# Extra TensorE products in a fused encoder: ahead of attention, in the last scan group, about its output product and at the feed-forward's entry

## The reference

```python
def reference(...):                      # 16 sequences, 36 image patches + 77 text tokens, 256 wide
    h = _L0_tok_ref(x, ...)              # patches @ W_proj.T + bias + position
    h = concatenate([h, txt], axis=1)    # (16, 113, 256)
    h = h + _L0_attn_ref(_layernorm(h), ...)   # causal attention, 16 heads of 16
    h = h + _L0_ffn_ref(_layernorm(h), ...)    # top-1 of 8 experts (256-512-256) + a shared expert
    h = h + _L1_attn_ref(_layernorm(h), ...)   # selective scan, below
    h = h + _L1_ffn_ref(_layernorm(h), ...)    # 704 hidden units, fake-quantised, below
    return h

def _L1_attn_ref(x, ...):
    x_in, res = jnp.split(x @ in_proj_w.T + in_proj_b, 2, axis=-1)
    xc = _silu(conv4(x_in))                                   # causal, 4 taps, per channel
    delta, Bp, Cp = jnp.split(xc @ x_proj_w.T + x_proj_b, [64, 80], axis=-1)
    delta = jax.nn.softplus(delta @ dt_proj_w.T + dt_proj_b)
    dA = jnp.exp(delta[..., None] * -jnp.exp(A_log))          # 16 states
    dBu = delta[..., None] * Bp[:, :, None, :] * xc[..., None]
    ys = scan(dA, dBu)                                        # over time
    y = ((ys * Cp[:, :, None, :]).sum(-1) + xc * D_param) * _silu(res)
    return y @ out_proj_w.T + out_proj_b + (x @ skip_proj_w.T + skip_proj_b)

def _L1_ffn_ref(x, ...):     # quantised to whole numbers: x, w_gate, w_up, then silu(gate)*up, w_down
    scale = sigmoid(clip) * max(abs(x)) / 127                 # one maximum over the whole tensor
    ...
```

## Time and profile before

| | us |
|---|---|
| median of 3 runs | 802.52 |
| lowest, highest | 800.22, 802.92 |
| profiled execution, first to last instruction | 798.0 |
| PE busy in it | 685.9 |
| DVE busy | 491.1 |
| ACT busy | 385.6 |
| POOL busy | 328.9 |

### The profile page before, as it was taken

How to read it: one execution, slowest core, us unless ns; L and a number is a source line. 1 busy time by engine, 2 the same in 40 slices (tenths; PEclk the granted TensorE clock), 3 DMA queues, 4 the chain that set the end, 5 groups by cost and what they waited for, 6 DMA issues and landing times. The chain is left out here.

```text
span 798.0 us, 11738 instructions
## 1 busy us (share of the span) xinstructions
PE 685.9 (86%) x3705; PEld 462.7 (58%) x3706; DVE 491.1 (62%) x885; ACT 385.6 (48%) x859; POOL 328.9 (41%) x310
## 2 busy tenths in 40 slices
PE   7599999997999979999996678898898896544886
PEld 5478888876666646666664556566566563312434
DVE  1556666665421114444225778898888988995586
ACT  0466666663222113333322666766766855211965
POOL 0012211110185403322321078878878878620337
PEclk9799999997799989999998899999999998865799
DMA  9993000000021261111114201202202202000003
GB/s 256 317 424 134 0 0 0 0 2 1 0 38 25 40 204 41 40 50 42 41 39 107 94 29 66 95 8 87 94 1 93 94 0 94 0 0 0 1 2 93
DMA packets 28836, 52.89 MB, mean 66 GB/s; under 512 B 10975, under 2 KB 23683, under 8 KB 26627
## 3 DMA queue, kind: packets, MB, share of 16 engines
q1 hardware_dynamic: 20067, 47.62, 17.8%
q0 software_dynamic: 8736, 4.85, 2.5%
HBM read 42.75 MB, written 9.60 MB: 66 GB/s over the span
## 5 line engine op out<-in xcount | busy, mean ns | idle before, releaser
L494 POOL TENSOR_TENSOR arena<-arena 128x904 f32<-128x904 f32 x64 | 124.8, 1950 | 66.6 <-DVE arena L1271 59.2
L1271 DVE TENSOR_TENSOR_SCAN arena<-ps,arena 128x452 f32<-128x452 f32 x128 | 133.7, 1087 | 11.6 <-POOL arena L494 4.4
L794 ACT ACTIVATE ps<-arena,sh_w 128x448 f32<-128x448 f32 x128 | 79.2, 632 | 94.9 <-DVE arena L1271 94.4
L1569 PE MATMUL ps<-arena,work 128*128 x176 | 83.4, 598 | 0.0
L569 ACT ACTIVATE work<-ps,work 113x113 f32<-113x113 f32 x256 | 66.8, 387 | 32.4 <-DVE work L928 32.4
L1261 DVE TENSOR_TENSOR arena<-arena,ps 128x904 f32<-128x904 f32 x64 | 69.0, 1079 | 12.8 <-PE ps L1744 12.7
L433 POOL TENSOR_TENSOR xT<-work 128x452 f32<-128x452 f32 x16 | 15.1, 942 | 139.1 <-DVE work L917 139.1
L542 POOL DMA_INDIRECT answers_e<-work,slot_token x22 | 23.6, 1073 | 100.6 <-DVE work L1066 100.6
L1762 PE MATMUL ps<-arena,const 128*128 128x452 f32 x96 | 49.4, 643 | 14.8 <-POOL arena L494 14.8
L526 POOL DMA_INDIRECT slots_in<-xn,slot x16 | 37.8, 2364 | 58.8 <-issue 58.8
L1757 PE MATMUL ps<-arena,const 128*128 128x452 f32 x80 | 40.7, 591 | 24.8 <-POOL arena L498 24.7
(11 more groups left out here) (247 smaller groups left out, 1377.9 us busy)
## 6 DMA issues: line engine op xcount, KB each, us to landing
arena<-c_rows SPq DMA_DIRECT2D x8, 1808.0 KB, 6.4
arena<-in_ex_w SPq DMA_DIRECT2D x8, 1536.0 KB, 23.5
slots_in<-work SPq DMA_DIRECT2D x1, 2827.0 KB, 23.6
work<-slots_in SPq DMA_DIRECT2D x22, 128.5 KB, 2.1
xn<-answers_e SPq DMA_DIRECT2D x4, 448.0 KB
out<-resid SPq DMA_DIRECT2D x8, 224.0 KB
arena<-in_patches SPq DMA_DIRECT2D x3, 576.0 KB, 6.1
sh_w<-in_sh_w SPq DMA_DIRECT2D x1, 1536.0 KB, 11.8
```

What stands on the lines that cost most here:

```text
L494: pool.tensor_tensor(read[kp], state[kp], c_all[par][:, 2 * c:2 * c + 2, :].unsqueeze(2).broadcast_to([P, 2, KT, N]), ALU.mult)\
L794: act.activation(decay_ps(n)[:, :, 1:], delta[par].rearrange("p k (b s) -> p (k b) s", b=GB)[:, :, 1:], ACT.Exp, scale=a_neg[:, 2 * c + n: ...
L1271: dve.tensor_tensor_scan(state[kp][:, n].rearrange("p k s -> p (k s)"), decay_ps(n).rearrange("p q s -> p (q s)"), drive[kp][:, n].rearran ...
L1569: last = pe.matmul(ps[:, bank, :], xgT[par][:, k, :], arena[:, bass.ds(e * EW + at + k * HID, HID)], start=k == 0, stop=k == KT - 1)
```

## The change

A helper `warm` issues bf16 products of the identity (128 by 128) with itself, repeated to 512 columns, into a bank that nobody reads at that time. It is called in eight places on PE: 24 products between the patch turns and the first sequence, with the wait for the cast of the identity moved ahead of the other waits; 6 at the end of every chunk of group 7; 4 between the last reduction and the output product; 26 between the output product and the maximum's turn; 4 between that turn and the spreading of the scale; 12 behind it; 3 ahead of each of the second to fourth turns of the quantised input. That is 127 products. No other engine's list is changed.

```diff
--- before.py
+++ after.py
@@ -56,6 +56,7 @@
 OPENING = 1
 AT_SKIP = (3, 4)
 FILL = (19, 2, 4)
+WARM_START, WARM_CHUNK, WARM_GATE, WARM_NORM, WARM_SCALE, WARM_ROUND, WARM_TURN = 24, 6, 4, 26, 4, 12, 3
 FIRST_SEQS, OTHER_SEQS = slice(0, GB), slice(GB, B)
 BUT_ONE_SEQS, ONE_SEQ = slice(0, B - 1), slice(B - 1, B)
 ROUTER_BANKS = (0, 1, 3, 4)
@@ -1336,6 +1337,10 @@
             dve_ffn(dve)
 
 
+        def warm(pe, bank, products):
+            for _ in range(products):
+                pe.matmul(ps[:, bank, :], identb[:, :], identb[:, :].unsqueeze(1).broadcast_to([P, 4, P]), start=True, stop=True)
+
         def pe_tokens(pe):
             h = B // 2 * IMG
             for part in range(PK // 2):
@@ -1454,8 +1459,9 @@
                 if back:
                     turn_back(b - 1)
 
+            pe.wait_ge(cast_done, 4)
+            warm(pe, 0, WARM_START)
             pe.wait_ge(attn_in, ATTN_LOADS * 16)
-            pe.wait_ge(cast_done, 4)
             pe.wait_ge(pool_set, 7)
             pe.wait_ge(img_ready, B // 2)
             turn_x(0, after_v=False)
@@ -1640,11 +1646,16 @@
             def scales(turn, parts):
                 pe.wait_ge(amax_ready, turn + 1)
                 pe.transpose(ps[0:1, 7, 0:parts], amax[0:parts, :], ident[0:parts, 0:parts]).then_inc(amaxT_ps, 1)
+                if turn == 0:
+                    warm(pe, 6, WARM_SCALE)
                 pe.wait_ge(scale_ready, turn + 1)
                 pe.matmul(ps[:, 7, 0:2], ones, amax1[:, 1:3], start=True, stop=True).then_inc(scale_ps, 1)
 
             scales(0, S)
+            warm(pe, 6, WARM_ROUND)
             for g in range(FG):
+                if g > 0:
+                    warm(pe, 6, WARM_TURN)
                 pe.wait_ge(xq_ready, g + 1)
                 for k in range(KT):
                     if g > 1:
@@ -1811,6 +1822,8 @@
                         if before:
                             pe.wait_ge(resid3_ready, g)
                         skip(g, par, AT_SKIP.index(c))
+                    if not more:
+                        warm(pe, 0, WARM_CHUNK)
 
             pe.wait_ge(diag_done, KT * (TAPS + 1))
             pe.wait_ge(pick_done, 1)
@@ -1834,7 +1847,9 @@
             step(GROUPS - 2, 0, turn_next=False)
             step(GROUPS - 1, 1, more=False, turn_next=False)
             reduce(GROUPS - 1, CHUNKS - 1, 1)
+            warm(pe, 0, WARM_GATE)
             project_out(GROUPS - 1)
+            warm(pe, 0, WARM_NORM)
 
         @block.tensor
         def _(pe):
```

## The result

The changed kernel took 790.31 us (median of 6 launches, 789.58 to 795.12), the kernel before 801.93 on the same chip (median of six; one of them took 3700.66 us and resembles no other, and without it the median is 801.35, from 800.22 to 802.92). The ratio is 0.9882, 95% interval 0.985 to 0.9914: faster by 1.2%, where 0.65% was forecast and the range ended at 794.6. With the launches of the later comparisons, and without that one, there are 71 of before (median 801.1, 795.6 to 805.6) and 18 of after (median 790.6, 789.5 to 795.4). The means, 801.2 and 791.9, stand 9.2 us apart, the medians 10.5.

The account below looks back on a forecast made before the run. DVE sets group 7; slow PE work matters only on the chain of waits: opening, end of group 7, feed-forward entry. Terms sum to -5.2 us: span 798.0 to 792.8, plus 4.5 gives 797.3 us, range 794.6 to 800.7.

Parts of the forecast that it names:

- The opening's -1.8: Opening of attention: 24 products fit PE's wait and L1375 and L1368 run at the high level; -1.8 us.
- the twelve and the threes: Feed-forward entry: 12 products (2.62 us) hide in a 3.04 us wait; each 3 (0.65 us) fit between turns.
- DVE was not held up: Last scan group: chunk products fit the slack before DVE's L1261; counted 0, bounds 0 to +1.3 us.
- it started low in this trace, so I go near that row: -0.4: Last reduction (last L1762): chunk products speed it up only a little; -0.4 us, bounds 0 to -1.68.
- a low period lifts the next, a high one loses it: Chunks of the last group: 1.5 us idle after low work lifts the clock, above 4 us after high loses it.
- rival 1: High all the way: chunk products hold 2.4 GHz into the last reduction; -7.2 us, 795.3 us, chance 0.13.
- The output product and its 26: L1778 speeds up as the clock rises inside the reduction, four products or its first half, -1.3; the 26 cost +0.1.
- L1662 gave -2.03 for -1.4: Feed-forward's first product: L1662 starts high, so DVE's third L1171 waits less; -1.4 us.
- ScalarE's seven passes: Behind L1662's start: seven passes of about 0.64 us each would end at 749.2 to 749.4.
- 4.5 us around the span: Whole run: the 798.0 us span lies 4.5 below the median time; the same 4.5 was added to 792.8.
- rival 3: Opening of attention: its gain does not arrive because another wait takes its place; -3.4 us, 799.1 us, chance 0.05.
- rule on turns: Feed-forward entry: by the Trainium skill, transposes don't count as busy for the clock, leaving only nine products between turns.

Follow-up runs that it names:

- e6: The full change without the 4, 12 and 3 x 3 products at the feed-forward's entry; 795.45 us, ratio 0.9908 against the kernel before.
- f2: The full change with 48 products at the opening in place of 24; 794.8 us, ratio 0.9932 against the kernel before.
- e2: The kernel before plus only the six products at each chunk's end in the last scan group; 798.99 us, ratio 0.998.
- e3: The kernel before plus only the products from the output product on (4, 26, 4, 12, 3 x 3); 799.19 us, ratio 0.9974.
- e1: The kernel before plus only the opening's 24 products; 797.54 us, ratio 0.997.
- e4: The full change without the chunk products; 793.86 us, ratio 0.9921 against the kernel before.
- e5: The changed kernel run again, unedited; 793.44 us, ratio 0.9893 against the kernel before.
- e7: The full change plus ten products ahead of the router's first turns; 790.72 us, ratio 0.987 against the kernel before.
- f3: The full change plus ten products ahead of the router's first turns, run once more; 791.21 us, ratio 0.9872 against the kernel before.
- f4: The changed kernel run a third time, unedited; 790.09 us, ratio 0.9878 against the kernel before.
- e8: e7 plus two wide products behind every third sequence's narrow router scores; 794.33 us, ratio 0.9894 against the kernel before.
- f1: The full change with twelve products per chunk of the last scan group in place of six; 795.63 us, ratio 0.9943 against the kernel before.

## Why the prediction was right in kind and too small in size

**The mechanism held at the opening and the entry.** Products in the waits bring the slow work there to the high level. L1364 to L1398 takes 14.3 us in every profile with the opening's 24 products but e6 (15.2) and f2, which has 48, and 16.3 in all without them (before, e2, e3). L1673 to the third L1172 takes 5.1 us in every profile with the entry's products, and 6.4 to 7.2 in all without (before, e1, e2, e6). The opening's -1.8 was -1.94; the twelve and the threes were hidden; DVE was not held up. At the output product the gain came too, but it isn't shown to come from the products put there: e2 has L1789 at 1.98 us with the chunk products alone, e1 with none there, and where the reduction runs low the four begin low with it and delay L1789 by 0.77 us (e3, e4). What the 4 and the 26 are worth beside the chunk products was not run.

**The step that failed: the last reduction, "it started low in this trace, so I go near that row: -0.4".** With the four products beside it I had -0.1; it was -1.60. The prediction had the products' effect in its own words (a low period lifts the next, a high one loses it) and then took nearly the value of the kernel without them. Every profile with six chunk products and the rest as well shows the last reduction high: 1.78 or 1.79 us in after, e5, e6, e7, f2, f3 and f4 (2.45 in e8, which changes the router as well). Without chunk products it was low in all four profiles (3.38, 3.35, 3.38 and 3.38 in before, e1, e3 and e4). The six products at 710.35 ran high and cut the wait before the last reduction from 4.12 us to 2.81, and the level held. In the kernel before it was high from 714.6 to 718.0 and fell in that wait, 1 us ahead of the reduction. Why it held at the last reduction and not at the one before stays open: the reduction at 707.23 waited only 2.62 us and took 3.28, behind one that was low as well, which the alternation of e2 doesn't explain. For the last reduction and the output product this is rival 1 and its size (-1.68, -1.87), but not "high all the way": two of the last three reductions were low.

**Two more terms too small.** The output product and its 26 gave -1.77 for -1.2, since the product was high from its first record. L1662 gave -2.03 for -1.4. There I had ScalarE's seven passes run one behind the other at 0.64 us each, the length of one in the earlier trace rows. In the timeline of after six of them, from L709 at 736.68 to L709 at 739.81, start 3.13 us apart, 0.52 each: they overlap, and length was taken for spacing. The difference is 6 x 0.12 = 0.7 us, as large as what was missing.

**The base.** I put 4.5 us around the span. Nearly every launch here has 1.8 to 2.2 us between its span and its time (2.5 to 2.9 in three): the profiled launch took about 800.0 us, a little faster than the median, and the 4.5 mixed its luck with the overhead. That matters less than it seems, since the sum in effect started from the median of three launches, 802.5, and the 71 average 801.2: 1.3 us too high. From 801.2 the prediction's sum gives 796.0, and the measured terms of the places touched (-1.94 - 5.34 = -7.3) give 793.9, where the 18 launches average 791.9.

**Scatter left out.** Two profiles of the changed kernel (after and f4) have spans of 788.3 and 788.2, that of e5 793.0; 11 of the 18 launches lie from 789.5 to 792.0, the other 7 from 792.5 to 795.4. Time goes with the mean granted clock of the launch (in e5's six, 0.951 goes with 790.4 and 0.942 with 794.85). The long launches that were profiled, e5 and e6, are those with the patches early (L1364 at 19.18 and 19.47); after, f4 and e4 have it at 20.33 to 20.35, the clock held at 39 and the router's low stretch was short. That is a correlation of five profiles, not a cause shown, and f3 speaks against it: patches at 20.25, clock held at 39, and yet the long stretch (198.3 to 208.5) and a span of 791.7. So rival 3, the opening's gain given back, is true of some launches; on the mean e1's -2.4 us says that it arrives.

**What stays open.** The places touched account for 7.3 us, the means differ by 9.2. The rest may be that the change shifts how often the router's stretch is short, or scatter of the samples. For the first: the stretch lasts 10.2 to 10.3 us in all three profiles without the opening's products (before, e2, e3), and with them 3.4 in five (after, e4, f1, f2, f4) and 6.8 in e1, but 10.2 or 10.3 in e5 and e6. Single blocks give -0.3%, -0.2% and -0.26%, together -0.76%, the full change -1.1 to -1.2%; each interval is 0.2 to 0.3% wide on either side, and by the means the single blocks give -3.6, -2.3 and -2.8 us, -8.8 together, against -9.2. So it is not shown that the blocks help one another in time. The rows speak against it at the output product, where e2 alone has the whole gain.

**Of the rule on turns.** From 729.25 to 733.97 PE did four groups of bf16 turns with three products between them, and the clock was 1.00 throughout. The Trainium skill ("TensorE: Matmul & The Clock Gate", Part 4: PE-mode transpose) says that they do not count as busy in the same way; with these products among them it made no difference here, and e6, which had turns without products, was at 0.50 there, but already had been as they began. For f32 turns e7 has the row: from 190.5 to 194.0 PE did nothing else, at 0.51, and from 194.0 the level was 1.00. There the measurement speaks against the Trainium skill's sentence, at least for this type. bf16 turns alone stay untested.

## What to carry to other kernels

Read the granted clock beside the waits: slow work at the low level on the path, with idle time ahead of it, can be bought back by unread products that fit into that idle time, here 0.217 us each at the high level and 0.43 at the low (the four of e3, 723.01 to 724.72). Products that overrun the wait cost what they overrun (48 for 24: 4.2 us; 12 for 6: DVE waits 1.5), so size them to the wait at the high level, and look one wait further back to see at which level they begin: low ones overran a wait of 0.73 us by 0.77 and took back part of the gain (e3, e4). Take the overhead around a span from launches that have both, and ask how far two launches of the same kernel lie apart before you set a range.

## What was not expected of the hardware

The clock also falls while PE never pauses: before at 199.2, behind 3.20 of 3.20 us busy from 195.9 on, and in e7 at 197.4, behind 3.40 of 3.40. PE came from turns of 113 columns and scores of 8 columns in both. In e5 at 39.0 it fell about a microsecond behind waits of 1.08 and 0.58 us, and stayed low for 3.4 us of unbroken work; in after the same waits (1.07 and 0.58) did not cost it. In the scan groups it falls for 3.4 us once in each of the six groups between 454 and 640 us, in before and in after; in e4 and f2 it did so in three, and each time it did not e4 gained about 1.2 us on after. That launch reached the last reduction 3.2 us ahead of after's and lost the lead in the tail. At the end of the program the clock fell in every launch profiled, in some at the last moment (before, after, e5, e6, e7, f2, f3, f4) and in others early enough to slow the last products (e1 to e4, e8, f1), which is worth 1.4 us and in f1 2.3. The rows are the busy time by stretch of after and then of e4, the same 186 us of groups:

```profile
454.40:640.00 185.60, 162.76 (x646) 109.44 (x645) 158.58 (x165) 124.31 (x237) 147.33 (x103) 0.94 0.16 61
```

```profile
454.40:640.00 185.60, 161.84 (x662) 107.69 (x662) 161.61 (x169) 125.27 (x239) 150.23 (x104) 0.97 0.16 61
```

This makes a single profile's span uncertain by several microseconds, more than any one block here was worth.
